# FFN weights asked for after the last turned probabilities, and the last row tile finished before tile 14, in an attention + int8 FFN layer kernel on eight cores

## The reference, cut to what matters

```
x = layernorm(x + attn(x))          # 16 heads of 128
x = layernorm(x + ffn(x))

attn: q1,k1,q2,k2,v = x @ W.T per head
      out = (softmax(q1 k1/sqrt(128)) - lam * softmax(q2 k2/sqrt(128))) @ v ;  out @ o_w.T
ffn:  q, in_scale = int8 quantisation of each token by its largest absolute value
      fp16((q @ weight.T) * in_scale * w_scale + bias)
```

## Time and profile before

| | us |
|---|---|
| median of 3 runs | 2298.63 (2297.24 to 2299.39) |
| profiled execution | 2296.81 |
| its span, slowest core (7) | 2295.3 |
| spans of the eight cores | 2283.9 to 2295.3 |
| PE busy | 2223.4 (97%) |
| DVE busy | 1366.7 (60%) |
| ACT busy | 1313.8 (57%) |
| POOL busy | 239.7 (10%) |

### The profile page before, as it was taken

One profiled execution on the slowest core, in us unless ns is written; L12 is line 12 of the kernel. 1 busy time (PEld: TensorE's weight loads), 2 busy tenths in 40 slices (PEclk: granted clock), 3 DMA queues, 4 the chain that ended last, 5 costly groups with the idle time before them and its releaser, 6 DMA issues.

```text
span 2295.3 us, 32951 instructions; the slowest of 8 cores (2283.9 to 2295.3 us)
## 1 busy us (share of the span) xinstructions
PE 2223.4 (97%) x10240; PEld 1003.0 (44%) x10240; DVE 1366.7 (60%) x1939; ACT 1313.8 (57%) x2308; POOL 239.7 (10%) x545
## 2 busy tenths in 40 slices
PE   6999999999999999999999999999999869999996
PEld 2444444444444444444444444444444324444443
DVE  1366666666666666666666666666666645655555
ACT  0276666666666666666666666666667632333332
POOL 3000000000000000000000000000001042322222
PEclk9999999999999999999999999999999989999998
DMA  9898677676668676776876766767579792433332
GB/s 143 110 139 122 112 123 119 106 124 116 115 106 127 102 127 109 122 124 105 128 115 108 122 116 106 132 108 116 102 155 197 134 254 82 136 109 110 116 114 72
DMA packets 701802, 280.05 MB, mean 122 GB/s; under 512 B 634560, under 2 KB 683712, under 8 KB 701120
## 3 DMA queue, kind: packets, MB, share of 16 engines
q1 hardware_dynamic: 644448, 197.32, 45.2%
q0 software_dynamic: 57184, 80.62, 23.1%
HBM read 156.77 MB, written 33.03 MB: 83 GB/s over the span
## 4 chain that ended last, share of the span: by engine, by line
PE 89%; DMA 5%; DVE 2%; issue 1%; POOL 1%; ACT 1%; SPq 0%; POOLq 0%; DVEq 0%; ACTq 0%
PE psP L332 45%; PE psS L351 19%; PE psO L363 9%; PE psS L678 7%; PE psO L685 4%; PE psP L685 4%; DMA xw<-xT 2%; DMA dt<-p 2%; DMA wr<-wqkv 1%; DMA qT<-qb 1%; ACT p L446 1%; PE psO L318 0%; SPq L281 0%; ACT dump L731 0%; PE psP L389 0%
## 5 line engine op out<-in xcount | busy, mean ns | idle before, releaser
L446 ACT ACTIVATE p<-psS 128x1024 bf16<-128x1024 f32 x1024 | 1048.5, 1025 | 578.4 <-PE psS L351 570.9
L332 PE MATMUL psP<-xw,wr 128*128 128x512 bf16 x4800 | 1192.6, 379 | 0.5 <-DVE qk L460 0.5
L332 PEld LDWEIGHTS psP<-xw,wr 128*128 128x128 bf16 x4800 | 469.6, 98 | 567.1 <-issue 1.0
L351 PE MATMUL psS<-qk 128*128 128x512 bf16 x2048 | 611.1, 380 | 7.9 <-ACT p L446 7.8
L476 DVE SCALAR_TENSOR_TENSOR p<-p,gg 128x2048 bf16<-128x2048 bf16 x256 | 602.0, 2351 | 27.4 <-DVE p L474 1.0
L460 DVE CAST qk<-psP 128x512 bf16<-128x512 f32 x245 | 168.6, 688 | 256.3 <-PE psP L332 255.5
L351 PEld LDWEIGHTS psS<-qk 128*128 128x128 bf16 x2048 | 200.0, 98 | 253.3 <-issue 17.0
L363 PE MATMUL psO<-dt,vv 128*128 128x512 bf16 x1024 | 264.4, 382 | 11.7 <-DMA dt<-p 11.5
L223 POOL DMA_DIRECT2D wr<-wqkv x75 | 56.2, 749 | 1452.8 <-PE psP L332 1390.6
L446 ACT ACTIVATION_READ_ACCUMULATOR p<-psS 128x1 f32 x1024 | 199.5, 195 | 0.0
L474 DVE TENSOR_SCALAR p<-p,rr 128x2048 bf16<-128x2048 bf16 x256 | 190.6, 745 | 0.0
(11 more groups left out here) (91 smaller groups left out, 903.8 us busy)
## 6 DMA issues: line engine op xcount, KB each, us to landing
wr<-wqkv POOLq DMA_DIRECT2D x75, 512.0 KB, 8.0
out<-xr SPq DMA_DIRECT2D x32, 512.0 KB, 2.9
xr<-x SPq DMA_DIRECT2D x13, 1024.0 KB, 5.7
xw<-xT POOLq DMA_DIRECT2D x16, 512.0 KB, 13.5
wob<-wo POOLq DMA_DIRECT2D x16, 512.0 KB, 10.7
xw<-wob POOLq DMA_DIRECT2D x16, 512.0 KB, 6.3
osc<-ot SPq DMA_DIRECT2D x60, 128.0 KB, 2.7
wfb<-wffn POOLq DMA_DIRECT2D x12, 512.0 KB, 13.5
```

What stands on the lines that cost most here:

```text
L332: mm = te.matmul(psP[:, (g % 2) * 512:(g % 2) * 512 + 512], wr[:, (i % WSLOTS) * 2048 + c * 128:(i % WSLOTS) * 2048 + (c + 1) * 128], xw[: ...
L351: mm = te.matmul(psS[k % 2][:, n * 512:(n + 1) * 512], q, qk[h % 2][:, k0:k0 + 512], start=True, stop=True)
L446: sc.activation(out, psS[k % 2][:], AF.Exp, scale=INV_SQRT_HD, accum_out=acc[:, (s % 4) * 4 + j:(s % 4) * 4 + j + 1]).then_inc(sEXP, 1)
```

## The change

- POOL asks for the FFN weights (all 16 chunks) only after the last four `dt` transposes have landed, the last V is turned and block 62 is done: chunks 0 to 3, `first(0)`, chunks 4 to 7, `first(1)`, chunks 8 to 15, `first(2)`, `first(3)`.
- POOL's loads within the last head are moved: `woload` 12 to 15 to the starts of steps 0, 0, 1, 2 (before: 12 to 14 at once, 15 at step 3), `ocfirst(1)` from step 3 to 4, `xload(1)` from 5 to 7, `ocfirst(2)` from 8 to 10, `xload(2)` and `ocfirst(3)` from 9 to 12.
- DVE does `add_x(3)` ahead of `quantise(1)`.
- The last tile's mean and 1/std get columns of `stp`, and a semaphore of their own. ACT does all squares of tile 15, its square root and its half of the normalising ahead of normalising tile 14; SP stores tile 15 ahead of tile 14.

```diff
         def moments(e, tick, n, scol, col, late=0):
             e.wait_ge(sSQ, 2 * n)
-            m, x2 = mv[:, 0:1], mv[:, 1:2]
-            var, r0, t = (lv[:, col + j:col + j + 1] for j in range(3))
-            r, nb = lv[:, col + 4:col + 5], lv[:, col + 5:col + 6]
+            mx, lx = (stp[:, 0:4], stp[:, 4:10]) if late else (mv[:], lv[:, col:col + 6])
+            m, x2 = mx[:, 0:1], mx[:, 1:2]
+            var, r0, t, sd, r, nb = (lx[:, j:j + 1] for j in range(6))
...
-            e.tensor_scalar(nb, t, -1.0, None, OP.mult).then_inc(sRN, 1)
+            e.tensor_scalar(nb, t, -1.0, None, OP.mult).then_inc(sRE if late else sRN, 1)
...
-            for c in range(12, 15):
+            for c in range(12, 16):
+                at_step(HC, (c - 12) * 3 // 4)
                 woload(c)
-            at_step(HC, 3)
-            woload(15)
+            at_step(HC, 4)
             ocfirst(1)
-            at_step(HC, 5)
+            at_step(HC, 7)
             xload(1)
-            at_step(HC, 8)
+            at_step(HC, 10)
             ocfirst(2)
-            at_step(HC, 9)
+            at_step(HC, 12)
             xload(2)
             ocfirst(3)
-            at_step(HC, NT)
-            g.wait_ge(sVT, vturned(HC))
-            g.wait_ge(sPV, NB * HC)
-            for c in range(6):
-                wfload(c)
-            g.wait_ge(sPV, NB * H - 1)
-            for c in range(14, 16):
-                wfload(c)
-            g.wait_ge(sD, NSTEP)
-            for c in range(11, 14):
-                wfload(c)
...
             tick(g.memset(lv[:, 15:16], -0.5))
-            first(0)
             for j in range(4):
                 g.wait_ge(sDT[j], 16 * NSTEP // 4)
-            for c in range(6, 11):
+            g.wait_ge(sVT, vturned(HC))
+            g.wait_ge(sPV, NB * H - 1)
+            for c in range(4):
+                wfload(c)
+            first(0)
+            for c in range(4, 8):
                 wfload(c)
             first(1)
+            for c in range(8, NC_):
+                wfload(c)
             first(2)
             first(3)
...
-                store(i)
+                store(i if i < NT - 2 else 2 * NT - 3 - i)
...
                 if i == NT - 2:
                     last_squares(NT - 1, 0, 0, 1024)
+                    last_squares(NT - 1, 1, 1024, 1536)
+                    last_squares(NT - 1, 2, 1536, 2048)
+                    sc.wait_ge(sVAR, 1)
+                    sc.activation(stp[:, 7:8], stp[:, 4:5], AF.Sqrt).then_inc(sSD, 1)
+                    sc.wait_ge(sRE, 1)
+                    y = xr[(NT - 1) % 4][:, 0:1024]
+                    sc.activation(y, y, AF.Identity, scale=stp[:, 8:9], bias=stp[:, 9:10]).then_inc(sNH, 1)
                 normalise(i, 0, last_moment(i), 8, sNL)
                 normalise(i, 1, last_moment(i), 8, sNL)
...
-            last_squares(NT - 1, 1, 1024, 1536)
-            last_squares(NT - 1, 2, 1536, 2048)
-            sc.wait_ge(sVAR, 1)
-            sc.activation(lv[:, 11:12], lv[:, 8:9], AF.Sqrt).then_inc(sSD, 1)
-            normalise(NT - 1, 0, 2 * NT, 8, sNL)
...
             quantise(0)
-            quantise(1)
             add_x(NPRE, 0)
             add_x(NPRE, 1)
+            quantise(1)
             quantise(2)
```

More of the change, by code:

```diff
@@ L135, in build_program @@
         sTQ = sems("sTQ0", "sTQ1")
-        sA, sF, sZ, sSQ, sQ, sZ2, sVC, sNF, sNL, sNE, sVAR, sSD, sRN, sGC, sFE = sems(
-            "sA", "sF", "sZ", "sSQ", "sQ", "sZ2", "sVC", "sNF", "sNL", "sNE", "sVAR", "sSD", "sRN", "sGC", "sFE")
+        sA, sF, sZ, sSQ, sQ, sZ2, sVC, sNF, sNL, sNE, sNH, sVAR, sSD, sRE, sRN, sGC, sFE = sems(
+            "sA", "sF", "sZ", "sSQ", "sQ", "sZ2", "sVC", "sNF", "sNL", "sNE", "sNH", "sVAR", "sSD", "sRE", "sRN", "sGC", "sFE")
         scale_all = E(nc.sbuf_tensor("scale_all", [128, NT], F32))
@@ L498, in moments @@
             e.wait_ge(sSQ, 2 * n)
-            m, x2 = mv[:, 0:1], mv[:, 1:2]
-            var, r0, t = (lv[:, col + j:col + j + 1] for j in range(3))
-            r, nb = lv[:, col + 4:col + 5], lv[:, col + 5:col + 6]
-            tick(e.tensor_tensor(mv[:, 2:4], st[:, scol:scol + 2], st[:, scol + 2:scol + 4], OP.add))
-            tick(e.tensor_scalar(mv[:, 0:2], mv[:, 2:4], INV_D, None, OP.mult))
+            mx, lx = (stp[:, 0:4], stp[:, 4:10]) if late else (mv[:], lv[:, col:col + 6])
+            m, x2 = mx[:, 0:1], mx[:, 1:2]
+            var, r0, t, sd, r, nb = (lx[:, j:j + 1] for j in range(6))
+            tick(e.tensor_tensor(mx[:, 2:4], st[:, scol:scol + 2], st[:, scol + 2:scol + 4], OP.add))
+            tick(e.tensor_scalar(mx[:, 0:2], mx[:, 2:4], INV_D, None, OP.mult))
             tick(e.tensor_tensor(t, m, m, OP.mult))
@@ L508, in moments @@
                 e.wait_ge(sSD, late)
-                tick(e.reciprocal(r0, lv[:, col + 3:col + 4]))
+                tick(e.reciprocal(r0, sd))
             else:
@@ L635, in store @@
                 for half in range(2):
-                    if i == NT - 1 and half == 1:
-                        sy.wait_ge(sNE, 1)
+                    if i == NT - 1:
+                        sy.wait_ge(sNE if half else sNH, 1)
                     else:
@@ L828, in add_ffn @@
                 c = 8 + 4 * (i % 2) + 2 * k
-                if i >= 2:
+                if 2 <= i:
                     ve.wait_ge(sNL, 2 * (i - 1))
@@ L868, in _ @@
             moments(ve, settle, 2 * NT, 12, 8, 1)
-            ve.wait_ge(sRN, 2 * NT)
+            ve.wait_ge(sRE, 1)
             y = xr[(NT - 1) % 4][:, 1024:2048]
-            ve.tensor_scalar(y, y, lv[:, 12:13], lv[:, 13:14], OP.mult, OP.add).then_inc(sNE, 1)
+            ve.tensor_scalar(y, y, stp[:, 8:9], stp[:, 9:10], OP.mult, OP.add).then_inc(sNE, 1)
     return nc
```

## The result

| | before | changed |
|---|---|---|
| median | 2298.63 us, 3 runs | 2281.91 us, 4 runs (2279.09 to 2283.04) |
| ratio to before, 95% interval | | 0.9933 (0.992 to 0.9945) |
| profiled execution | 2296.81 | 2281.14 |
| its spans | 2283.9 to 2295.3 | 2264.1 to 2279.6 |
| mean span of the eight cores | 2287.8 | 2272.5 |

The kernel is faster, by 17 us between the medians and 15.7 between the profiled executions, not by the 31 us forecast: 2281.9 us lies above the range of 2261 to 2278.

What follows compares the result with a forecast made beforehand. PE's idle stretches ahead of `ffn(0)`, in core 7's last head and the tail were taken as the bound. Core 0: 2287.1 - 21.8 - 1.1 = 2264.2, plus 1.5 and 1.8 gives 2267.5 us; range 2261 to 2278.

Steps and rivals of the forecast that it cites:

- Part 1: Ahead of block 63: with no weights beside it the last transpose takes 4.3 us, not 20.65, so PE's wait goes.
- the sum for `ffn(0)`: From the last fill through block 63 and two output projections: `ffn(0)` starts 22.1 us earlier, 21.8 on core 0.
- Part 2: Ahead of `outproj(4)`: `add_x(3)` ahead of `quantise(1)` on DVE removes PE's idle 6.34 us.
- What is late next: At `ffn(0)`: turned tile 0, weights and POOL's list come in time; no stall taken, bounded by 0 and 5 us.
- The bound of 20.65 us for `qtrans(0)`: At `ffn(0)`: if tile 0's transpose took 20.65 us instead of 13.7, it would land 2.8 us late.
- The rival priced a late chunk: At `ffn(0)`: weights or `qtrans(0)` are late by up to 5 us, giving 2272.5 us; chance 0.17.
- Part 3: Loads in the last head: moving them costs 0 and gains 8.2 us on core 7, nothing on core 0.
- the stall stays: In the last head: PE's stall remains on some core in most runs, median 2275.4 us; chance 0.27.
- the sum for the slowest core: Span ends after all gains: core 0 at 2264.2, core 7 at 2263.9; slowest taken as 2264.2 us.
- Part 4: Behind PE's last product: finishing tile 15 ahead of normalising tile 14 gains 1.1 us.
- taken back later: Around `ffn(0)` and `ffn(1)`: DVE's list runs late and about half the gain is lost, 2279 us; chance 0.04.
- slower: At `ffn(0)`: the eight last weight chunks land 42 us late against 23.2 won, 2317 us; chance 0.03.

Runs made afterwards that it cites:

- e3: The changed kernel with the FFN weights asked for as before, eleven chunks ahead of the end of the transposes; median 2289.4 us.
- e5: The changed kernel with `add_x(3)` put behind `quantise(1)` again, as before; median 2295.1 us.
- e1: The changed kernel with the loads of the last head put back to their steps of before; median 2277.4 us.
- e2: The kernel before with only the loads of the last head moved; median 2297.5 us.
- e8: The changed kernel with FFN weight chunks 0 to 7 asked for ahead of `first(0)` and 8 to 15 behind it; median 2274.7 us.
- e4: The changed kernel with the end as before, tile 14 normalised and stored ahead of tile 15; median 2283.5 us.
- e7: The changed kernel with output weights 12 to 15 all asked for at the start of the last head; median 2277.3 us.

## Why the prediction was wrong

The slowest core was forecast at 2264.2 and is core 1 at 2279.6, 15.4 us later: the last fill 7.8 us later than the 1842.3 of core 0 that the sum took, 7.3 us from `ffn(0)` to PE's end, 0.3 at the end and nothing in between. The 1.8 us added for the median came to 0.8.

- **Part 1, the transpose, and the sum for `ffn(0)`: right.** 4.3 us, no wait, full pace; 31.3 us from the last fill on five cores, 31.8 on average, against the 31.1 to 31.3 of the sums. e3 shows that the weights were the reason.
- **Part 2: right**, and 21.9 us measured for both parts against 21.8 to 22.1. The prediction did not say that part 1 makes part 2 needed; e5 shows it.
- **"What is late next", the weights: the failed step.** The slack of 2.3 us was made of rates read in stretches where one queue ran alone (350 and 419 GB/s) and of 4.3 us for the transpose. Side by side they ran at 265 to 302. And the sum had bytes move at full rate from 1855 on, where the rate was 111 to 1858: it put nothing between the issue of a load and its first packet, which for chunk 4 was 5.6 us. On core 7, whose last fill came 2.9 us earlier than in the sum, chunk 7 landed at 1876.8 (forecast 1868.7), `qtrans(0)` at 1878.1 (1877.9), the last chunk at 1889.2 (1885). The bound of 20.65 us for `qtrans(0)` came true on core 5, where it took 20.0 us and `ffn(0)` waited 2.27.
- **The two rules of the Trainium skill.** That transposes are as fast as other DMAs ("Advanced Engine Details and Errata", section "X-Bar Transpose (TRN2)") did not hold here: 512 KB took 4.3 us alone and 16.3 beside weights, against 2.7 for a 512 KB store alone. Going by it would have made the weights look safer still. That POOL cannot write descriptors beside fast fp32 work of DVE ("SBUF — State Buffer", section "SBUF: two separate sides") shows in no issue time: 3.11 us for four and 6.06 for eight, 0.8 each. Chunk 4, though, had its first packet 5.6 us behind its issue on core 1. DVE was at work on fp32 data in the second half of that time, but idle for the first 2.2 us of it (0.00 from 1855 to 1857), and a start like chunk 0's (1.3 to 2.2 us) would have come within these; whether the rule explains the rest was not tried.
- **What a wait costs: mis-sized.** The rival priced a late chunk at up to 5 us. The wait is 4.03 us on core 1, but the stage grows by 7.3 us: the granted clock is 0.50, the lower of its two levels, in the stretch behind it, and the next 8 products take 3.57 us where 8 take 1.89.
- **Part 3, cost 0 and a gain of 8.2 us: wrong in sign, the other failed step.** It looked at the one load that had been slow, and not at what the new places of the others lie beside. Output weights 14 and 15 now come in steps 1 and 2, where a transpose is under way each time, and steps are short. Cost 2.8 us of mean span (e1, e2; 1.0 to 1.3 beside e8's weights), and the stall that was to vanish from the slowest core came to more cores. The rival "the stall stays" had its mechanism right, with too few cores. The reading of before was short as well: core 2 waited 4.35 us for ACT in its last head, so the stall was not on core 7 alone. And the sum for the slowest core looked at cores 0 and 7 only; core 2, at 2291.0 us before, comes to 2268.1 by the same gains.
- **Part 4, 1.1 us: mis-sized**, 0.4 to 0.5 by e4, 0.3 between before and changed. ACT is through 0.5 us earlier against PE's end (13.1 instead of 13.6 us). But four stores now follow each other, and the last takes 4.3 us to land, where it took 3.5:

```profile
2272.66 2.92 SPq L635 DMA_DIRECT2D out<-xr  x4
```
```profile
out<-xr SPq DMA_DIRECT2D x1, 512.0 KB, 4.3
```

- **The range** held each rival alone (2275.4; 2272.5 and more) but not both, and both came. They were priced as if one excluded the other, though they lie on different stretches of PE; added up by their own prices they give 2280.4, near the 2281.9 measured.
- The rivals "taken back later" and "slower" did not come: behind `ffn(1)` the distances were those of before.

## What to carry to other kernels

When a load is moved, look at what stands beside it in its new place, and take the rate from a stretch in which the same two queues run together; a rate of a queue alone is a bound. Ask for a big load as soon as its memory is free and before its queue runs dry, ahead of small computations on the engine that issues it. With the slowest of eight cores as metric, a stall that comes now and then on any core is paid nearly always, so count it on all cores and compare mean spans.

## What the runs showed of the hardware

- A 512 KB transpose issued beside output weight 14 or 15 took 6.8 to 17.9 us in the changed kernel, alone 4.3. On core 7 89 to 131 GB/s were moved from 1752 to 1760, where in single microseconds of 1744 to 1751 the transpose alone moved up to 291 and the weights alone up to 344. Why is open.
- Two DMA queues took turns packet by packet where 1 KB packets ran beside 256 byte, 2 KB or 8 KB ones, so small packets lose bytes to large ones. It is not so everywhere: in the last head, on core 7 from 1754 to 1756, 15 packets of 4 KB (output weights) stand against 690 of 256 bytes (transpose).
- A load had its first packet 1.3 to 2.2 us (chunk 0) or 4.2 to 5.6 us (chunk 4) behind its issue in the changed kernel. Why the second is longer is open.
- A wait of PE of 4.0 us was followed by about 6 us of slow products, at a granted clock of 0.50 to 0.70, which cost 3.3 us more (core 1 of the changed kernel); one of 2.5 us (core 6) cost 0.2 more, one of 2.3 us (core 3 of e7) 1.9 more.
